# Self-attention P.V with high and low halves of V in one operand, in a decoder layer on one core

## The reference, cut to what matters

```python
q = (x @ Wq.T).reshape(b, t, H, DH).transpose(0, 2, 1, 3)
k = (x @ Wk.T).reshape(b, t, HKV, DH).transpose(0, 2, 1, 3)
v = (x @ Wv.T).reshape(b, t, HKV, DH).transpose(0, 2, 1, 3)
...
scores = jnp.einsum('bhgtd,bhkd->bhgtk', qg.astype(jnp.float32), k.astype(jnp.float32)) / math.sqrt(DH)
scores = jnp.where(causal[None, None, None], scores, jnp.finfo(jnp.float32).min)
attn = jax.nn.softmax(scores, axis=-1).astype(x.dtype)
ctx = jnp.einsum('bhgtk,bhkd->bhgtd', attn, v)
out = ctx.reshape(b, H, t, DH).transpose(0, 2, 1, 3).reshape(b, t, E)
return out @ Wo.T
```

## Time and profile before

| what | value |
|---|---|
| median of three runs | 1008.93 us |
| the profiled execution, its own time | 1010.24 us |
| span of its records (first to last instruction) | 1008.5 us |
| granted TensorE clock, mean | 0.998 |
| TensorE (PE) busy | 996.3 us, 99% |
| VectorE (DVE) busy | 641.1 us, 64% |
| ScalarE (ACT) busy | 558.6 us, 55% |
| GpSimd (POOL) busy | 519.5 us, 52% |
| one batch of the self-attention (batches 0 to 6) | 29.8 to 29.9 us |

### The profile page before, as it was taken

The page is one execution under the profiler, slowest core; times in us unless marked ns, Lnnn a source line. Parts: engine busy times, 40 slices in busy tenths (PEclk is TensorE's granted clock), DMA queues, the critical chain, the costliest instruction groups (busy, mean ns, idle before and its releaser), DMA issues.

```text
span 1008.5 us, 16102 instructions
## 1 busy us (share of the span) xinstructions
PE 996.3 (99%) x5552; PEld 837.9 (83%) x5552; DVE 641.1 (64%) x1224; ACT 558.6 (55%) x1695; POOL 519.5 (52%) x529
## 2 busy tenths in 40 slices
PE   8999999999999999999999999999999999999997
PEld 7777777777788888888888888888888888799996
DVE  6888888888433786555555555555555567656654
ACT  4766666666533665565656556556655667522221
POOL 3645444444231787665765756566666568412220
PEclk9999999999999999999999999999999999999999
DMA  9400111103454213223213323322332245100000
GB/s 331 129 22 22 43 42 43 43 22 109 141 159 125 94 54 105 73 95 105 78 70 105 105 64 104 91 78 94 95 105 75 84 146 170 50 22 21 21 21 21
DMA packets 74857, 85.15 MB, mean 84 GB/s; under 512 B 4512, under 2 KB 54688, under 8 KB 74784
## 3 DMA queue, kind: packets, MB, share of 16 engines
q1 hardware_dynamic: 74784, 84.21, 26.2%
HBM read 65.32 MB, written 18.87 MB: 83 GB/s over the span
## 4 chain that ended last, share of the span: by engine, by line
PE 93%; DVE 3%; ACT 1%; issue 1%; DMA 1%; POOL 1%; DVEq 0%; POOLq 0%; SPq 0%; ACTq 0%
PE bank L237 23%; PE bank L239 22%; PE bank L238 22%; PE bank L1143 11%; PE bank L1187 5%; PE bank L903 3%; PE bank L864 1%; PE bank L868 1%; PE bank L871 1%; PE bank L874 1%; DMA rawKV<-in_L_attn_Wv_dram 1%; DVE Kbdl L1696 0%; ACT Pb L1424 0%; PE bank L817 0%; PE bank L810 0%
## 5 line engine op out<-in xcount | busy, mean ns | idle before, releaser
L673 POOL TENSOR_TENSOR Pb<-Pb,b_rec 128x512 f32<-128x512 f32 x128 | 135.2, 1057 | 200.1 <-DVE b_rec L1848 200.1
L1424 ACT ACTIVATE Pb<-bank,b_nb 128x256 f32<-128x256 f32 x256 | 118.9, 476 | 15.1 <-DVE b_nb L1843 15.0
L1843 DVE TENSOR_REDUCE b_nb<-bank 128x2 f32<-128x512 f32 x128 | 88.0, 688 | 59.2 <-PE bank L239 58.4
L635 POOL TENSOR_TENSOR Pa<-Pa,a_rec 128x512 f32<-128x512 f32 x64 | 68.2, 1066 | 102.1 <-DVE a_rec L1727 101.5
L1342 ACT ACTIVATE Pa<-bank,a_nb 128x128 f32<-128x128 f32 x256 | 90.5, 368 | 45.6 <-DVE a_nb L1721 44.8
L1285 ACT ACTIVATE PTh<-bank 128x512 fp32r<-128x512 f32 x128 | 76.3, 596 | 67.3 <-PE bank L1187 67.3
L237 PE MATMUL bank<-WOh,Oh 128*128 128x512 f32 x256 | 111.4, 435 | 0.0
L1597 DVE TENSOR_TENSOR PTl<-bank,PTh 128x512 fp32r<-128x512 f32 x128 | 87.7, 685 | 21.7 <-ACT PTh L1285 21.6
L239 PE MATMUL bank<-WOh,Ol 128*128 128x512 f32 x256 | 101.1, 395 | 0.0
L238 PE MATMUL bank<-WOl,Oh 128*128 128x512 f32 x256 | 100.4, 392 | 0.0
L1285 ACT ACTIVATE Oh<-bank 128x512 fp32r<-128x512 f32 x64 | 38.3, 598 | 91.7 <-PE bank L239 91.7
(11 more groups left out here) (279 smaller groups left out, 3014.7 us busy)
## 6 DMA issues: line engine op xcount, KB each, us to landing
KV<-kv_scratch SPq DMA_DIRECT2D x64, 512.0 KB, 3.3
kv_scratch<-KVst SPq DMA_DIRECT2D x64, 256.0 KB, 3.1
raw<-in_L_xattn_Wo_dram SPq DMA_DIRECT2D x32, 256.0 KB, 3.7
raw<-in_L_xattn_Wq_dram SPq DMA_DIRECT2D x24, 256.0 KB, 3.2
cx<-in_ctx_dram SPq DMA_DIRECT2D x8, 256.0 KB, 9.5
raw_first<-in_L_xattn_Wq_dram SPq DMA_DIRECT2D x8, 256.0 KB, 4.5
raw<-in_L_ffn_up_w_dram SPq DMA_DIRECT2D x8, 256.0 KB, 3.9
raw<-in_L_ffn_down_w_dram SPq DMA_DIRECT2D x8, 256.0 KB, 3.3
```

What stands on the lines that cost most here:

```text
L635: gp.tensor_tensor(pj, pj, a_rec[:, SG * j:SG * j + SG].unsqueeze(2).to_broadcast([P, SG, P]), ALU.mult).then_inc(g_norm, 1)
L673: gp.tensor_tensor(pk, pk, b_rec[:, k % 4, :].unsqueeze(2).to_broadcast([P, 2, KEYS]), ALU.mult).then_inc(b_g_norm, 1)
L1424: op = act.activation(Pb[:, k % 4, h, :], bank[k % 3][:, h * KEYS:(h + 1) * KEYS], ACT.Exp, bias=b_nb[:, k % 4, h:h + 1], scale=1.0, accum ...
L1843: dve.tensor_reduce(b_nb[:, k % 4, :], bank[k % 3][:].rearrange("p (h k) -> p h k", h=2), AX.X, ALU.max, negate=True).then_inc(b_v_nb, 1)
```

## The change

V now stands in one operand, Vst. For j below 4 the high half of head j stands in the 16 columns at 16 j of its block and the low half 64 columns further on, for j of 4 and more the high half stands at 16 j and the low half 64 columns before. Two products per j (with PTah and with PTal) then give the high sums in one half of a bank's rows and the low sums in the other. Heads 0 to 3 add up in bank 7, heads 4 to 7 in bank 4. The low sums are rounded to fp32r by ScalarE (OLa, OLb), and a product with swap_r (an identity matrix with its halves exchanged, 64 rows high) adds them to the rows of the high sums: `add_low(0)` and `add_low(1)`. ScalarE and VectorE then split the result in two pieces of 64 rows each. The unit at the end of a batch is cut in two: its first two kcs stand before the Wo product, the others after it. The transposed keys move from bank 4 to bank 3. Of all four partial products of the halves, low by low is now computed as well.

```diff
-        Vbdh = sb("Vbdh", "F", 0, [SKV * VBW], F32R)
-        Vbdl = sb("Vbdl", "F", 4.5, [SKV * VBW], F32R)
-        OTh, OTl = PTah[:, 0, :], PTal[:, 0, :]
+        Vst = sb("Vst", "F", 0, [SKV, P], F32R)
+        OTh = sb("OTh", "F", 4, [D], F32R)
+        OTl = sb("OTl", "F", 6, [D], F32R)
+        swap_r = sb("swap_r", "ST", 6, [P], F32R)
+        LOWER, UPPER = slice(0, 64), slice(64, P)
+        OLa, OLb = OTl[UPPER, :], PTah[LOWER, 0, :]
...
# SyncE
-            sp.wait_ge(pe_pv, NB)
+            sp.wait_ge(pe_wo, NB)
...
# TensorE, scores
-                for bk, _ in halves:
+                for n, (bk, _) in enumerate(halves):
+                    if m == 0 and n:
+                        pe.wait_ge(v_qkl, 2 * b + 2)
+                    if m == 1 and n == 0 and b:
+                        pe.wait_ge(v_ol, 2 * b)
                     pe.matmul(bk[:].rearrange("p (c k) -> p c k", c=SG), ident_r[:],
                               mask_r[:].unsqueeze(1).to_broadcast([P, SG, P]), start=True, stop=False)
...
# TensorE, values
-                    op = split3(pe, bank[7][:], Vbdh[:, j * P:(j + 1) * P], Vbdl[:, j * P:(j + 1) * P],
-                                PTah[:, j % 2, :], PTal[:, j % 2, :], j == 0, False)
+                    pe.matmul(bk[:], Vst[:, j, :], PTah[:, j % 2, :], start=j % 4 == 0, stop=False)
+                    op = pe.matmul(bk[:], Vst[:, j, :], PTal[:, j % 2, :], start=False, stop=j == 3)
+                    if j == 3:
+                        op.then_inc(pe_pv, 1)
+
+                def add_low(n):
+                    pe.wait_ge(a_ol, 2 * b + n + 1)
+                    bk, rows, low = ((bank[7], UPPER, OLa), (bank[4], LOWER, OLb))[n]
+                    pe.matmul(bk[:], swap_r[rows, :], low, start=False, stop=True,
+                              skip_group_check=True).then_inc(pe_sw, 1)
...
# TensorE, end of a batch
+                    if j == 6:
+                        add_low(0)
...
+                add_low(1)
+                tail = U_E0 - 1 if last else U_B0 + 2 * b + 1
+                pe.wait_ge(v_ol, 2 * b + 1)
+                unit(tail, (0, 1))
+                pe.wait_ge(v_ol, 2 * b + 2)
                 for g in range(SG):
...
-                unit(U_E0 - 1 if last else U_B0 + 2 * b + 1)
+                unit(tail, (2, 3))
...
# ScalarE
+                    if j == 5:
+                        act.wait_ge(pe_pv, 2 * b + 1)
+                        hi(OLa, bank[7][UPPER, :]).then_inc(a_ol, 1)
+                    if j == 7:
+                        act.wait_ge(pe_sw, 2 * b + 1)
+                        hi(OTh[LOWER, :], bank[7][LOWER, :]).then_inc(a_o, 1)
...
-                act.wait_ge(pe_pv, b + 1)
-                hi(OTh, bank[7][:]).then_inc(a_o, 1)
+                act.wait_ge(pe_pv, 2 * b + 2)
+                hi(OLb, bank[4][LOWER, :]).then_inc(a_ol, 1)
                 if not last:
                     values_hi(b + 1)
+                act.wait_ge(pe_sw, 2 * b + 2)
+                hi(OTh[UPPER, :], bank[4][UPPER, :]).then_inc(a_o, 1)
...
# VectorE
+                        dve.wait_ge(a_o, 2 * b + 1)
+                        lo(OTl[LOWER, :], bank[7][LOWER, :], OTh[LOWER, :]).then_inc(v_ol, 1)
...
-                dve.wait_ge(a_o, b + 1)
-                for n, done in enumerate((v_ol_half, v_ol)):
-                    cols = slice(n * KEYS, (n + 1) * KEYS)
-                    lo(OTl[:, cols], bank[7][:, cols], OTh[:, cols]).then_inc(done, 1)
+                dve.wait_ge(a_o, 2 * b + 2)
+                lo(OTl[UPPER, :], bank[4][UPPER, :], OTh[UPPER, :]).then_inc(v_ol, 1)
```

More of the change, by code:

```diff
@@ L815, in turn_k @@
                 pe.wait_ge(v_qr, 2 * b + 2)
+                if b:
+                    pe.wait_ge(a_exp, SKV * b)
                 for m in range(KC):
-                    op = pe.transpose(bank[4][:, m * P:(m + 1) * P], kr[:, m * P:(m + 1) * P], ident[:])
+                    op = pe.transpose(bank[3][:, m * P:(m + 1) * P], kr[:, m * P:(m + 1) * P], ident[:])
                 op.then_inc(pe_qk, 1)
@@ L907, in values @@
                 def values(j):
+                    bk = bank[7] if j < 4 else bank[4]
                     if j == SKV - 1:
@@ L912, in values @@
                             cols = slice(n * KEYS, (n + 1) * KEYS)
-                            op = split3(pe, bank[7][:, cols], Vbdh[:, j * P:(j + 1) * P], Vbdl[:, j * P:(j + 1) * P],
-                                        PTah[:, j % 2, cols], PTal[:, j % 2, cols], False, n == 1)
+                            pe.matmul(bk[:, cols], Vst[:, j, :], PTah[:, j % 2, cols], start=False, stop=False)
+                            op = pe.matmul(bk[:, cols], Vst[:, j, :], PTal[:, j % 2, cols], start=False, stop=n == 1)
                         op.then_inc(pe_pv, 1)
@@ L1021, in _ @@
             unit(1)
-            pe.wait_ge(v_c, 4)
+            pe.wait_ge(v_c, 5)
             scores(0, 0)
@@ L1313, in k_hi @@
                 act.wait_ge(pe_qk, 2 * b + 2)
-                hi(KTh[:], bank[4][:].rearrange("p (k n) -> p k n", k=KC)).then_inc(a_qk, 1)
+                hi(KTh[:], bank[3][:].rearrange("p (k n) -> p k n", k=KC)).then_inc(a_qk, 1)
             def context_hi(b):
@@ L1367, in batch @@
                     k_hi(b + 1)
-                act.wait_ge(pe_pv, b + 1)
-                hi(OTh, bank[7][:]).then_inc(a_o, 1)
+                act.wait_ge(pe_pv, 2 * b + 2)
+                hi(OLb, bank[4][LOWER, :]).then_inc(a_ol, 1)
                 if not last:
                     values_hi(b + 1)
+                act.wait_ge(pe_sw, 2 * b + 2)
+                hi(OTh[UPPER, :], bank[4][UPPER, :]).then_inc(a_o, 1)
+                if not last:
                     for j in range(3):
@@ L1681, in values_lo @@
                 dve.wait_ge(a_v, b + 1)
-                vv = [t[:].rearrange("p (j c) -> p j c", c=VBW)[:, :, 0:SD] for t in (Vbdl, Vbdh)]
-                lo(vv[0], bank[0][:, P:2 * P].rearrange("p (j d) -> p j d", j=SKV), vv[1]).then_inc(v_vl, 1)
+                cells = Vst[:].rearrange("p a (b d) -> p (a b) d", d=SD)
+                for n in range(2):
+                    js = slice(4 * n, 4 * n + 4)
+                    first = 4 * n * (SKV + 1)
+                    at_lo = first + (-4 if n else 4)
+                    op = lo(cells[:, at_lo:at_lo + 3 * (SKV + 1) + 1:SKV + 1, :],
+                            bank[0][:, P:2 * P].rearrange("p (j d) -> p j d", j=SKV)[:, js, :],
+                            cells[:, first:first + 3 * (SKV + 1) + 1:SKV + 1, :])
+                op.then_inc(v_vl, 1)
             def q_lo(b):
@@ L1690, in k_lo @@
                 dve.wait_ge(a_qk, 2 * b + 2)
-                lo(KTl[:], bank[4][:].rearrange("p (k n) -> p k n", k=KC), KTh[:]).then_inc(v_qkl, 1)
+                lo(KTl[:], bank[3][:].rearrange("p (k n) -> p k n", k=KC), KTh[:]).then_inc(v_qkl, 1)
             def diagonal_keys(b, ms):
```

16 lines of the change are left out of this document (8 added, 8 removed).

## The result

| | before | changed |
|---|---|---|
| median of the runs (4 each, one chip) | 1008.83 us | 1021.02 us |
| ratio, 95% interval | 1 | 1.0121 (1.0108 to 1.0133) |
| profiled execution, its own time | 1010.24 us | 1021.63 us |
| batch 4, turn_latents to turn_latents | 29.85 us | 31.50 us |

The changed kernel is slower by 12.2 us; forecast were 6.5. The traces show where the 11.4 us between the two profiled executions lie: turn_latents of batch 0 starts 1.37 us later (71.59 against 70.22), the six batches after it hold 6 x 1.66 = 9.96 (until 260.61 against 249.28), and the last batch takes 42.75 us in both.

What follows compares the result with a forecast made beforehand. TensorE was taken as the bound, with four barely covered chains near a batch's end. Seven batches at +1.0 us and the last at -0.5 gave +6.5, 1016.7 us profiled or 1015.4 median; range 1008.2 to 1018.5.

Steps and rivals of the forecast that it cites:

- three waits: TensorE in a batch with a next one: some 0.4 us for PTal, 0.7 for KTl, 1.2 for xn2.
- the stretch up to turn(7): Values 0 to 5 save 1.38 us, add_low(0) costs 0.45, so turn(7) moves from 178.43 to 177.50.
- I take these gains whole: Up to turn(7): the 1.38 us saved and 0.45 spent count fully; the OLa wait costs at most a tenth.
- Products removed and added: TensorE, each batch: eight value products save 1.83 us, two permutation products cost 0.45 and 0.23, net -1.15.
- The wait at the second mask product: Half-height copies and subtractions ahead of the keys delay KTl; of 1.17 us gained, 0.7 is given back.
- Rival 2: 64-row copies cost half (1013.3) or the xn2 collision dissolves (1010.3); both together 1008.2; chance 0.14.
- The wait for xn2: Between Wo and turn_latents: a 4.07 us chain behind 2.92 us of cover, so 1.2 us idle per batch.
- The collision: xn2 on VectorE beside GpSimd's normalise on a shared port pair: 1.25 us kept; without it, 0.73 shorter.
- The last batch: Other products cover its waits: -1.15 us, some 0.6 back for add_low(1) and small waits, so -0.5.
- Rival 1: The waits don't appear and all products saved on TensorE count: net -9.2 us, 1000.4; chance 0.10.
- Rival 3: A further wait of scores(b + 1, 1) for its exponentials, 0.4 us more per batch: 1018.2; chance 0.10.
- Rival 4: Low sums come late and TensorE only trades one wait for another: no change, 1008.9; chance 0.06.

Runs made afterwards that it cites:

- Experiment 1: Kernel before the change, with only the last unit of a batch cut in two, half ahead of Wo: 1020.03 us, ratio 1.0106.
- experiment 9: Changed kernel with keys first, early high half of O, three next-unit products ahead of Wo, later add_low(0) and earlier reciprocals on VectorE: 1009.26 us.
- experiments 5 to 9: Changed kernel: six next-unit products ahead of Wo, 1018.82; plus keys first, high half early, 1014.18; three products, 1011.63; add_low(0) later, 1010.14; reciprocals earlier, 1009.26 us.
- experiment 11: Kernel of experiment 9 with the last sum of the rotated queries moved behind PTal(4) on VectorE: 1012.81 us, ratio 1.0042.
- experiment 2: Changed kernel with the unit at the end of a batch whole again behind Wo: 1025.83 us, ratio 1.0176.
- experiment 4: Changed kernel with OTh's upper rows copied before the low sums and three unit products ahead of Wo, not six: 1016.72 us.

## Why the prediction was right in its sign and short in its size

The mechanism was the forecast's: slower, by three waits, the largest for xn2. But 1021.02 lies above the range's end of 1018.5, and the step that failed is the sizing of four terms: the stretch up to turn(7), put 0.93 us shorter and 0.59 shorter in fact; Wo with the product ahead of the first pair; the handover to turn_latents; and the last batch, put at -0.5 and 0.0 in fact. Batch 4 of the changed kernel, shifted by 6.35 us so that both traces have turn_latents before it at the same time:

| step of the forecast | forecast | measured | miss added here |
|---|---|---|---|
| turn(7) | 177.50 | 177.84 | +0.34 |
| last values begin | 179.24 | 179.58 | 0 |
| second mask product | 180.76 | 181.10 | 0 |
| first pair | 181.09 | 181.53 | +0.10 |
| add_low(1) | 181.90 | 182.35 | +0.01 |
| Wo begins | 183.72 | 184.16 | -0.01 |
| Wo ends | 186.47 | 187.02 | +0.11 |
| turn_latents | 190.6 | 191.24 | +0.1 |

Together +0.65 in each batch. The seven batches with a next one hold 11.3 us instead of 7.0, the last batch 0.0 instead of -0.5, and 0.1 lies behind it. That makes the 4.9 us between 6.5 and 11.4.

- **"I take these gains whole"**, of values 0 to 5, was the largest slip. Turn(6), before and after:

```profile
176.74 0.60 PE L903 MATMUL bank<-ident,Pa 128*128 128x128 f32 x4
```

```profile
182.20 0.62 PE L918 MATMUL bank<-ident,Pa 128*128 128x128 f32 x4
```

  Five products fewer should have brought it to 176.74 - 5 x 0.23 = 175.59; it stands at 182.20 - 6.35 = 175.85, 0.26 later. On the way TensorE reached turn(3) and turn(6) before GpSimd had divided (weight loads idle for 0.29 and 0.24 us), and values(4) before PTal(4) was there (0.11). The forecast had looked only at the end of a batch.
- **Products removed and added.** The price of a permutation product among full-height ones was 0.45 and is 0.43. The wait for OLa was said to cost "at most a tenth" and put at nothing. ScalarE's rows:

```profile
181.79 0.60 ACT L1319 ACTIVATE PTah<-bank 128x512 fp32r<-128x512 f32 x1 [0.33 <-PE bank L918]
182.41 0.59 ACT L1319 ACTIVATE OTl<-bank 64x512 fp32r<-64x512 f32 x1
183.03 0.60 ACT L1319 ACTIVATE PTah<-bank 128x512 fp32r<-128x512 f32 x1
```

  The copy (OLa bears the name OTl) starts 0.62 behind the one before it, and the next 0.62 behind it, where PTah and KTh in the earlier trace rows stand 0.50 apart. add_low(0) so starts 0.53 behind turn_q, which took 0.45 before. From turn(6) to turn(7) are 1.99 us, forecast were 1.91: the other 0.08 of the 0.34.
- **The wait at the second mask product** was right to the hundredth in its place: 1.52 us from the last values, and the half-height subtraction costs a whole. The product behind the wait stands 0.43 from the first pair, not 0.33. Rival 2's first half, cheap copies of 64 rows, is excluded by the rows of VectorE and ScalarE.
- **Wo** was priced at 12 x 0.229 = 2.75, though the earlier trace rows show 182.46 to 185.31, 2.85, its first product taking 0.33. It was a misreading, not an unknown.
- **The wait for xn2** is the forecast's: the chain is 4.07, xn2 still 1.25, and only the handover to turn_latents is 0.15 and not 0.05. The collision did not dissolve, so rival 2's second half fell too. One reading of it was loose: what is left of GpSimd's 1.04 us when xn2 starts (189.10 - 188.13 = 0.97) plus 0.52 is 1.49, not 1.25, so the rows show a delay beside GpSimd's division but not that sum. Experiment 1 shows the uncovered chain alone.
- **The last batch.** That "none of the three waits lasts" failed for xn2:

```profile
302.74 0.39 PE L244 MATMUL bank<-XTh,WQl 128*128 128x512 f32 x1
303.36 0.63 PE L838 MATMUL bank<-ident,xn 128*128 128x128 f32 x4 [0.23 <-DVE xn L1843]
```

  Its turn_latents starts 0.62 us behind the product before it, where 0.23 is the usual distance. This 0.39 and the two permutation products (0.42 and 0.43) take two thirds of the 1.83 us that the eight products gave; the rest went in tenths.
- **TensorE's busy time** was to fall by some 2 us in a batch and fell by 0.2, since short waits count as busy time.
- **Rival 1** (1000.4) fell with the result, and even with the long waits gone, in experiment 9, the time is 1009.26. **Rival 3** did not appear: the second scores follow Wo at once, at 193.37. **Rival 4** fell with the result.
- **The range** was too narrow above, since it priced each error once for each wait but took the cheap stretch ahead of turn(7) as exact. An error of a tenth in each of four steps, seven times, is 3 us.

Why has experiment 9 nothing left of the gain? From one turn_latents to the next a batch is 31.3, 30.7, 30.2, 30.0 and 30.0 us long in experiments 5 to 9, and 29.85 before. Laid beside the kernel before product by product, the batch of experiment 9 loses 1.83 us of products. It gains 1.07 in the two permutation products (0.68 for the first with the wait for PTal behind it, 0.39 for the second) and 0.58 ahead of values(4), which start 0.94 behind turn(5) instead of 0.36 (175.61 to 175.97 before); the rest are tenths, at turn_k, the second mask product and the borrowed products. The row of values(4) names VectorE's PTal as what it waited for, and in batch 6, where VectorE has less to do, this wait is nearly gone. So VectorE's queue in the middle of the batch is what stood next in the way. (Batch 6 lacks one power on GpSimd too, and no run takes the two apart.) What stays open is whether it can be unburdened in the other batches: experiment 11 only moved the wait. A form without the two permutation products, with the low sums multiplied by a copy of Wo with its rows exchanged, was not tried; the high half of such a copy alone is 8 KB of SBUF in each partition.

## What to carry to other kernels

Where every chain around TensorE is covered by a tenth of a microsecond, removing products shortens the cover and not the chains: write down, for each wait that the removed work hid, how long its chain is and what is left to hide it, over the whole loop and not only at the edit. Filling work moved ahead of a product is taken from behind it; if both stretches lie in one serial chain, the batch is as long one way as the other (experiment 2 against the changed kernel). And a saving that must pass through two other engines and back pays their whole copies, at 64 rows as at 128.

## What the runs showed of the hardware that was not expected

- **The clock behind a short idle time.** In experiment 2 TensorE idled 1.41 us ahead of Wo in each of the eight batches. In two of them the granted clock then fell from 1.00 to 0.50 (from 2.4 to 1.2 GHz) for 3.4 us, which cost 1.6 us each; in the other six it stayed at 1.00, and so it did behind each 1.14 us ahead of turn_latents in the changed kernel. What TensorE did before looks alike in the seven batches with a next one: it idled 0.45 us for KTl, worked without a pause until 1.41 us before Wo, and stood still. The four executions had mean clocks of 0.991 to 0.996, so how often it falls varies.
- **Half height on ScalarE and VectorE costs what full height does**: copies 0.59, subtractions 0.67 to 0.69. In the rows looked at, a ScalarE copy that reads the rows from 64 on stands 0.62 from its neighbours in the queue (OLa above, and OTh's upper rows in experiment 4), where others stand 0.47 to 0.50 apart.
- **Who pays in a collision** turned with 0.1 us of order: Kbdl took 0.69 us just ahead of a Kbdh, and 1.52 just behind one.
